# Deformable convolution: one odd image spread and copied a step ahead, its product in two instructions

## The reference

```python
om = conv3x3(x, w_off) + b_off                      # 27 maps: 9 offsets y, 9 offsets x, 9 masks
py = off_y + row + ky;  px = off_x + column + kx    # where tap k of a pixel samples
sampled[c, k, h, w] = bilinear(x[c], py, px) * sigmoid(mask)
out = einsum('bckhw,ock->bohw', sampled, w) + b     # then batch norm, ReLU, + x
```

## Time and profile before

| | |
|---|---|
| time, median of 3 runs | 2334.54 us (2331.11 to 2341.95) |
| span of the profiled execution | 2334.2 us |
| main loop, first to last start of an odd product (L939) | 701.87 to 2102.41 us |
| PE matmul busy, whole span | 66% |
| DVE busy | 67% |
| ACT busy | 62% |
| POOL busy | 26% |
| HBM traffic over the span | 154 GB/s |

### The profile page before, as it was taken

How to read it: one execution, slowest core, us unless ns; L and a number is a source line. 1 busy time by engine, 2 the same in 40 slices (tenths; PEclk the granted TensorE clock), 3 DMA queues, 4 the chain that set the end, 5 groups by cost and what they waited for, 6 DMA issues and landing times. The chain is left out here.

```text
span 2334.2 us, 61913 instructions
## 1 busy us (share of the span) xinstructions
PE 1539.5 (66%) x24206; PEld 1050.0 (45%) x24207; DVE 1558.4 (67%) x1718; ACT 1449.8 (62%) x2219; POOL 606.7 (26%) x1168
## 2 busy tenths in 40 slices
PE   4755980000008888888898898898888898891620
PEld 4632330000006666666665566666665666660310
DVE  5342006656717888888888788888887888883105
ACT  2221224344218898888898898898887898890102
POOL 2000000000033444444443444444444444430000
PEclk9688995555558999999999999999999999996555
DMA  2177874667675666666666666566666656640008
GB/s 116 32 190 184 233 218 159 215 227 275 235 214 126 151 147 157 149 149 155 150 148 152 148 149 157 149 150 157 149 146 150 152 147 157 149 100 22 3 0 338
DMA packets 288861, 362.19 MB, mean 155 GB/s; under 512 B 61853, under 2 KB 260820, under 8 KB 285014
## 3 DMA queue, kind: packets, MB, share of 16 engines
q1 hardware_dynamic: 209552, 226.57, 37.6%
q0 software_dynamic: 36864, 59.94, 11.2%
q10 hardware_dynamic: 42182, 72.05, 9.0%
HBM read 253.94 MB, written 104.39 MB: 154 GB/s over the span
## 5 line engine op out<-in xcount | busy, mean ns | idle before, releaser
L758 POOL DMA_DIRECT2D rows<-scratch_parts x1152 | 583.1, 514 | 821.1 <-PE ps_even_y L790 798.8
L799 PE MATMUL ps_odd_y<-rows,sel 32*128 32x504 f32 (+2 forms) x928 | 459.8, 496 | 502.5 <-DMA rows<-scratch_parts 345.2
L939 DVE TENSOR_TENSOR G<-odd_y,ps_odd_v 128x1008 f32<-128x1008 f32 (+2 forms) x464 | 542.0, 1168 | 182.5 <-PE ps_odd_v L816 182.4
L816 PE MATMUL ps_odd_v<-tent_x,stage 32*128 32x171 f32 (+2 forms) x5568 | 591.1, 318 | 0.0
L947 DVE TENSOR_TENSOR G<-even_v,ps_even_y 128x1008 f32<-128x1008 f32 (+2 forms) x464 | 539.3, 1162 | 23.6 <-ACT even_v L895 21.7
L816 PE MATMUL ps_even_v<-tent_x,stage 32*128 32x171 f32 (+3 forms) x5568 | 541.9, 324 | 8.5 <-DMA stage<-scratch_xt 8.3
L889 ACT COPY odd_y<-ps_odd_y 128x504 f32<-128x504 f32 (+2 forms) x928 | 526.4, 567 | 21.4 <-PE ps_odd_y L799 17.1
L895 ACT COPY even_v<-ps_even_v 128x1008 f32<-128x1008 f32 (+2 forms) x464 | 450.2, 970 | 134.6 <-PE ps_odd_v L816 126.5
L834 PE MATMUL ps_r<-G,conv_w 128*32 128x224 f32 (+1 forms) x8832 | 483.3, 346 | 13.2 <-ACT res L900 13.1
L799 PEld LDWEIGHTS ps_odd_y<-rows,sel 32*128 32x128 f32 x928 | 173.0, 186 | 689.8 <-issue 350.5
L816 PEld LDWEIGHTS ps_odd_v<-tent_x,stage 32*128 32x128 f32 x5568 | 477.8, 190 | 0.0
(11 more groups left out here) (134 smaller groups left out, 913.5 us busy)
## 6 DMA issues: line engine op xcount, KB each, us to landing
place<-scratch_px SPq DMA_DIRECT2D x960, 105.0 KB, 3.4
scratch_parts<-parts ACTq DMA_DIRECT2D x18, 3136.0 KB, 16.7
rows<-scratch_parts POOLq DMA_DIRECT2D x960, 52.5 KB, 3.4
x<-scratch_xh SPq DMA_DIRECT2D x48, 406.0 KB, 5.9
place<-scratch_px SPq DMA_DIRECT2D x192, 84.0 KB, 2.7
scratch_om<-om ACTq DMA_DIRECT2D x64, 196.0 KB, 7.1
rows<-scratch_parts POOLq DMA_DIRECT2D x192, 42.0 KB, 2.6
scratch_conv<-res SPq DMA_DIRECT2D x448, 14.0 KB, 1.8
```

The lines of the kernel that those rows point to most:

```text
L758: pool.dma_start(bass.AP(tensor=rows[b][:].tensor, offset=32 * g * pitch + here, ap=[[2 * pitch, Y_KINDS], [GROUP * W, 3], [1, count * W]] ...
L799: nc.tensor.matmul(ps_odd_y[:, lo:hi], sel[32 * g:32 * g + 32, :], taps(rows, 32 * g, 32, p, lo, hi), start=True, stop=True).then_inc(odd_ ...
L816: m = nc.tensor.matmul(sub(ps_v[g // 2], 0, 128, i * 512 + lo + first, dims), stage[32 * g:32 * g + 32, j * IMAGE + v * C:j * IMAGE + (v + ...
L939: nc.vector.tensor_tensor(two(G, ROW, v, slot(v)), two(odd_y[p % 3], ROW, v), two(ps_v[1], 512, v), ALU.mult).then_inc(odd_weighted, 1)
```

## The change

PE: `spread_odd(p+1, 0)` moves out of the place behind `spread_even(p)` and into `sample(p)`, behind its first column block; the wait for the row tents (`rows_ready`) moves with it. `spread_odd(p+1, 1)` moves in front of `reduce`. Inside `sample`, the wait for the odd product of the step before no longer stands in front of everything: in the first column block g = 2 waits for the product of image 0 and g = 3 for that of image 1.

ACT: the copy of image 0's spread tents is made one step earlier. The order in step p becomes `keep_even(p)`, `keep_odd(p+1, 1)`, `distance(p+2)`, `keep_odd(p+2, 0)`, `result`. DVE: `weight_odd` is two instructions, one for each image, each behind the copy of its own image. The number of matmuls, copies and DMAs stays, DVE has one more instruction in each step, and the data computed are the same.

```diff
--- before.py
+++ after.py
@@ -799,18 +799,22 @@
                     nc.tensor.matmul(ps_odd_y[:, lo:hi], sel[32 * g:32 * g + 32, :], taps(rows, 32 * g, 32, p, lo, hi),
                                      start=True, stop=True).then_inc(odd_spread, 1)
 
-                def sample(it, p):
+                def sample(it, p, to):
                     n = STEPS * it + p
                     for c, (first, count) in enumerate(BANDS):
                         if p == max(0, (first - WIN + 1) // 2):
                             pe.wait_ge(stage_loaded[c], 16 * 4 * len(COLUMNS) * (it + 1))
                     pe.wait_ge(tent_ready, n + 1)
                     wait(pe, even_kept, n)
-                    wait(pe, odd_weighted, n)
                     for j, (x0, x_lo, x_hi) in enumerate(COLUMNS):
+                        if j == 1 and to:
+                            rows_ready(*to)
+                            spread_odd(*to, 0)
                         first, count = SPAN * j, min(SPAN, W - SPAN * j)
                         for g in range(4):
                             i, v = g % 2, 2 * p + g // 2
+                            if j == 0 and g >= 2:
+                                wait(pe, odd_weighted, 2 * n - 1 + i)
                             lo, hi = columns(v)
                             dims = [[W, (hi - lo) // W], [1, count]]
                             m = nc.tensor.matmul(sub(ps_v[g // 2], 0, 128, i * 512 + lo + first, dims),
@@ -846,17 +850,14 @@
                 def body(it, last):
                     for p in range(STEPS):
                         to = ahead(it, p + 1, last)
-                        sample(it, p)
+                        sample(it, p, to)
                         spread_even(it, p)
                         if to:
-                            rows_ready(*to)
-                            spread_odd(*to, 0)
+                            spread_odd(*to, 1)
                         if at := block_of(it, p):
                             if at[2] == 0:
                                 pe.wait_ge(even_weighted, STEPS * at[0] + BLOCK // 2 * (at[1] + 1) + 1)
                             reduce(*at)
-                        if to:
-                            spread_odd(*to, 1)
                 unrolled(PAIRS, body)
                 pe.wait_ge(even_weighted, STEPS * PAIRS)
                 for t in range(BLOCK // 2):
@@ -884,7 +885,7 @@
                     n = STEPS * it + p
                     act.wait_ge(odd_spread, 2 * n + i + 1)
                     if i == 0:
-                        wait(act, odd_weighted, n - 1)
+                        wait(act, odd_weighted, 2 * (n - 2))
                     lo, hi = columns(2 * p + 1)
                     nc.scalar.copy(odd_y[p % 3][:, i * ROW + lo:i * ROW + hi], ps_odd_y[:, lo:hi]).then_inc(odd_kept, 1)
 
@@ -903,16 +904,16 @@
                 keep_odd(0, 0, 0)
                 distance(0, 1)
                 keep_odd(0, 0, 1)
+                keep_odd(0, 1, 0)
 
                 def body(it, last):
                     for p in range(STEPS):
                         keep_even(it, p)
                         if to := ahead(it, p + 1, last):
-                            keep_odd(*to, 0)
+                            keep_odd(*to, 1)
                         if to := ahead(it, p + 2, last):
                             distance(*to)
-                        if to := ahead(it, p + 1, last):
-                            keep_odd(*to, 1)
+                            keep_odd(*to, 0)
                         if at := block_of(it, p):
                             if at[2] == BLOCK // 2 - 1:
                                 result(BLOCKS * at[0] + at[1])
@@ -934,10 +935,13 @@
                 def weight_odd(it, p):
                     n = STEPS * it + p
                     v = 2 * p + 1
-                    dve.wait_ge(odd_kept, 2 * n + 2)
+                    lo, hi = columns(v)
                     dve.wait_ge(sampled, n + 1)
-                    nc.vector.tensor_tensor(two(G, ROW, v, slot(v)), two(odd_y[p % 3], ROW, v),
-                                            two(ps_v[1], 512, v), ALU.mult).then_inc(odd_weighted, 1)
+                    for i in range(2):
+                        dve.wait_ge(odd_kept, 2 * n + 1 + i)
+                        nc.vector.tensor_tensor(sub(G, 0, 128, slot(v) + i * ROW + lo, [[1, hi - lo]]),
+                                                odd_y[p % 3][:, i * ROW + lo:i * ROW + hi],
+                                                ps_v[1][:, i * 512 + lo:i * 512 + hi], ALU.mult).then_inc(odd_weighted, 1)
 
                 def weight_even(it, p):
                     n = STEPS * it + p
```

## The result

The changed kernel takes 2317.71 us (median of 12 runs, 2306.74 to 2331.40) beside 2332.51 us of the kernel before, measured with it. The ratio is 0.9936, with a 95% interval of 0.9919 to 0.9953: some 15 us faster, where 42 were forecast. The profiled execution has a span of 2315.2 us; its main loop, counted from the first to the last even product on DVE, takes 1381.9 us where it took 1400.6.

What follows compares the result with a forecast made beforehand. Bound: a ring of PE and ACT, 2.94 us a step. 2334.2 - 73 + 16 + 10 + 5 + 3 = 2295, less some 3 us for short and first steps: 2292 us, range 2270 to 2315.

Steps and rivals of the forecast that it cites:

- The bound of the kernel before: Main loop: a PE-ACT ring of keep_even, first odd copy, spread load and sampling sets nearly all ordinary steps, 2.94 us.
- (a): PE and ACT, the ring with its copy halved: PE waits for the copy mid-sampling; ring 2.62 us, 0.32 less.
- (b): DVE's odd product in two instructions: 1.18 us in place of 1.12, +0.06; DVE's ring 2.62 us.
- (c): PE and ACT over two steps, through spread, reduction and sampling: 2.67 us a step, bounds 2.63 and 2.77.
- (d): Step that ends a block: reduction 0.38 longer, 3.05 us; four steps 11.06 against 11.76, 0.175 us a step, 73 us.
- (e): Waits for the products, moved inside the sampling: no cost, products end at 0.82 and 1.41, before the copy at 1.52.
- (f): SP's queue at changes of pair and near step 12: takes back 16 and 10 us, plus 5 for slow steps.
- (g): POOL's row tents, wanted about 0.9 us earlier: 3 us added for waits.
- a new wait replaces the old: Rival: ps_odd_y's single bank still handed back and forth, reduction later; 0.075 us a step, 2315 to 2325 us; chance 0.15.
- DVE's share: Sign: DVE over 90% busy in the main-loop stretch examined.
- the ordinary steps: Sign: 2.62 to 2.70 us between first odd products, one in four near 3.0; prediction wrong if above 2.85.
- the waits for the stores: Sign: ACT's wait for the stores up from 27.6 to about 50 us; prediction wrong if they don't grow.

Runs made afterwards that it cites:

- halves_only: The kernel before with only the odd product in two instructions and the row blocks' single waits, no spread, copy or reduction moved: 2333.0 us.
- short_copy0: The changed kernel, with image 0's copy of spread tents taking only half its columns from the seventh step on: 2306.1 us, four steps 11.02 us.
- short_tail: The changed kernel without the third column block of the sampling from the second pair of images on: 2320.8 us, four steps 11.61 us.
- spread_late: The changed kernel with the spread in the sampling one column block later, behind the second: 2443.5 us, four steps 12.77 us.
- early_result: The changed kernel with ACT's copy of a finished block moved in front of image 0's copy: 2353.8 us, ratio 1.0082 to the kernel before.
- one_product: The changed kernel with the odd product in one instruction again, behind both copies, and one wait for it in the sampling: 2316.1 us, four steps 11.61 us.

## Why the prediction was wrong

*The bound of the kernel before.* Right. The ring through `keep_even`, the first odd copy and the sampling was removed and the waits that named it fell; `halves_only`, which leaves the ring, changed nothing.

*(a) and (b)*, the ring with the copy halved (2.62) and DVE's (2.62): neither held the changed kernel. `short_copy0`, where the bank's ring is shortened, settles at 2.67, so their size is about right; no run tells them apart. DVE's +0.06 was measured as +0.07 (1.19 against 1.12). The estimate from the Trainium skill's page "VectorE: DVE Perf Modes" (section on the TRN2 errata), +0.125 us a step, was too high: the halves take 0.676 us each and start 0.60 us apart (median), so that they overlap by 0.08 us.

*(c) is the step that failed.* It followed ACT's last copy, the spread of image 1, the reduction and the sampling to the **sampling's end**, and stopped: 5.34, or 2.67 a step. It took the start of the copy of image 0 from ACT's own order, 2.11. But that copy's spread stands in the sampling, and the sampling stands behind the reduction. Its own numbers, followed on to the next spread of image 1, give the ring: the reduction ends at 4.14, the sampling begins at 4.08, the first block takes 0.3, the spread 0.50, the copy 0.04 + 0.58 + 0.05, so the spread of image 1 comes at 5.55 after 2.74: 2.81 us, and with (d)'s 0.38 for the third tap 3.19. Four steps are 3 x 2.81 + 3.19 = 11.62; measured are 11.61. A ring must be closed on the resource that it holds, here the bank; I had closed it on `sampled`. `short_copy0`, `short_tail` and `spread_late` show this ring from three sides. The sampling itself also became longer, 1.38 us from its first product to its end for the 1.27 of the kernel before (medians), with a spread in it; (c) had kept 1.26. The bounds of (c), 2.63 and 2.77, came from the same open chain, so the true 2.78 lay just outside them, and the time outside the forecast's own range of 2270 to 2315.

*(d)* The long step: 3.22 for 3.05, and the step behind it is late by 0.1 as well, since ACT copies the block just before `keep_even`; `early_result` took 0.05 us of this away and 0.06 of the long step. That was not in the forecast.

*(e)* Right: no cost and no gain (`one_product`).

*(f)* The mechanism was right, the size wrong both ways: nothing that can be seen was taken back from the real gain, and some 41 us would have been from the one forecast. So the forecast's 73 us of shorter steps would have come out near 32, not 42. Part of this could have been read beforehand: (f) counts a slow step of some 1.1 us extra in seven of the 15 changes of pair, but the trace of the kernel before has a step at a mean granted clock of 0.50 to 0.75 in steps 3 to 6 of 13 of them.

*(g)* PE's weight load for the odd spread waited 4.8 us for the row tents, 1.3 us in the same view of before: 3.5 us more, near the 3 us charged.

Put together: 0.04 us a step is 26 x 16 x 0.04 = 17 us, which is the main loop's 18.7 with the first five steps, at the lower clock (granted 0.50 from 700 to 720 us), each 0.36 shorter. Of the rivals the second came true, "a new wait replaces the old" through the handed-back bank, with the time of its first figure, 2315 to 2325. That the figure fits is luck in part: it took 0.075 us a step less 15 to 20 us for (f) and (g), and measured were 0.04 a step and next to nothing for (f). I gave it 0.15, and called it a matter of delays between four rings instead of working it out. Of the signs that were named, the wait for `odd_y`, DVE's share (90.3%) and the halves came true; the ordinary steps (2.72 to 2.88), the long one (3.22 for 3.0) and the waits for the stores did not, and the last was named as a sign that the prediction is wrong.

## What to carry to other kernels

When a step is moved so that it no longer waits for one engine, follow every buffer that it holds until it is free again: with a single bank handed between two engines, all that stands between two writes in program order is in the ring, even work that has nothing to do with it. An engine at 97% busy may still only be waiting; leaving out a third of the sampling, 17% of its instructions, showed it. And before a steady step is made shorter, look for a queue whose time doesn't shrink with it: one more small buffer gave this kernel 38 us, more than twice what the change did, and decided whether a further move gained 11 us or lost 36.

## What wasn't expected of the hardware

An idle time of PE costs more than itself. In `early_result` PE stood idle for 3.60 us, and the granted clock was 0.71 in the five microseconds around that and 0.61 in the five behind; over the pairs the two steps behind the wait took 0.53 and 0.67 us longer (medians). In the kernel before, such slow steps make up some 14 of the 42 us that the single buffer costs. And the four DMAs of a store, 14 KB each and issued in 1.7 us together, were waited for by ACT for up to 3.6 us: SP issues them behind groups of 12 loads, each 5 to 7 us of issuing, and a second buffer made the waits vanish.
